# A graph kernel's first attention: the exponential's argument of three units in ten formed by VectorE from two broadcast rows

## The reference

```python
h = (x @ W).reshape(N, H, C)
as_n = (h * a_src).sum(-1)
ad_n = (h * a_dst).sum(-1)
e = jax.nn.leaky_relu(as_n[src] + ad_n[dst], NEG_SLOPE)      # slope 0.2
m = jax.ops.segment_max(e, dst, num_segments=N)
p = jnp.exp(e - m[dst])
s = jax.ops.segment_sum(p, dst, num_segments=N)
alpha = p / (s[dst] + 1e-16)
out = jax.ops.segment_sum(alpha[:, :, None] * h[src], dst, num_segments=N)
```

## Time and profile before

| | |
|---|---|
| median of 3 runs | 3774.85 us (3772.26 to 3774.91) |
| the profiled execution | 3773.97 us, span 3772.4 us |
| first attention's units, from the first weighing to the last eviction | 602.09 to 1079.70 us of the span |
| busy in the whole span | TensorE 93%, VectorE 53%, ScalarE 45%, GpSimd 55% |

### The profile page before, as it was taken

One profiled execution on the slowest core, in us unless ns is written; L12 is line 12 of the kernel. 1 busy time (PEld: TensorE's weight loads), 2 busy tenths in 40 slices (PEclk: granted clock), 3 DMA queues, 4 the chain that ended last, 5 costly groups with the idle time before them and its releaser, 6 DMA issues.

```text
span 3772.4 us, 58635 instructions
## 1 busy us (share of the span) xinstructions
PE 3494.7 (93%) x19026; PEld 2954.7 (78%) x19027; DVE 1984.3 (53%) x2688; ACT 1694.6 (45%) x2961; POOL 2059.4 (55%) x1612
## 2 busy tenths in 40 slices
PE   7998867999988799779998999999999999999898
PEld 4565436999988799623334799999999999999898
DVE  7346888888643544699985442433342424240034
ACT  1114777888843331379994233333333333333221
POOL 7888885666657530000000477777777777776400
PEclk9999998999999999889999999999999999999999
DMA  4342112223143421411103577777777676765501
GB/s 149 108 117 70 33 33 77 79 80 92 53 123 100 129 65 56 137 54 38 42 29 124 187 174 168 171 172 167 174 165 176 164 176 161 180 161 108 104 32 66
DMA packets 171359, 423.60 MB, mean 112 GB/s; under 512 B 39614, under 2 KB 62165, under 8 KB 171222
## 3 DMA queue, kind: packets, MB, share of 16 engines
q0 software_dynamic: 69184, 193.10, 24.5%
q1 hardware_dynamic: 87702, 202.74, 16.5%
q10 hardware_dynamic: 14336, 26.07, 1.9%
HBM read 293.54 MB, written 127.92 MB: 112 GB/s over the span
## 4 chain that ended last, share of the span: by engine, by line
PE 46%; ACT 7%; DVE 2%; issue 2%; DMA 1%; SPq 0%; POOL 0%; ACTq 0%; DVEq 0%; POOLq 0%
PE ps L2156 31%; PE ps L2143 7%; ACT work L1342 4%; ACT ps L1333 3%; PE ps L1746 3%; PE ps L331 2%; PE ps L323 2%; DVE work L1164 1%; PE ps L1279 1%; DVE work L1192 1%; DMA ct<-x_d 0%; ACT work L1352 0%; PE ps L343 0%; DMA acc_d<-ct,relrec 0%; DMA hbuf<-acc_d 0%
## 5 line engine op out<-in xcount | busy, mean ns | idle before, releaser
L2156 PE MATMUL ps<-wsplit,xsplit 128*128 x6840 | 1234.8, 337 | 0.0
L2156 PEld LDWEIGHTS ps<-wsplit,xsplit 128*128 128x128 f32 x6840 | 1180.2, 188 | 0.0
L2196 ACT ACTIVATE ct<-ps,invs 128x768 f32<-128x768 f32 x190 | 171.3, 902 | 919.1 <-PE ps L2156 919.1
L2053 DVE CAST wsplit<-wplain 128x768 fp32r<-128x768 f32 x210 | 157.5, 750 | 804.6 <-PE ps L2156 788.1
L1342 ACT ACTIVATE work<-ps,work 128x418 f32<-128x418 f32 x720 | 438.5, 631 | 109.2 <-PE ps L1252 103.7
L1289 PE MATMUL ps<-hbuf,work 128*128 128x193 f32 x2400 | 455.4, 328 | 15.1 <-DVE work L1206 13.1
L2106 POOL DMA_INDIRECT acc_d<-ct,relrec x190 | 335.6, 1766 | 236.0 <-DMA acc_d<-ct,relrec 185.8
L2085 POOL TENSOR_TENSOR xsplit<-ct,xsplit 128x768 fp32r<-128x768 f32 x190 | 447.8, 2357 | 0.3 <-ACTq L2190 0.2
L1289 PEld LDWEIGHTS ps<-hbuf,work 128*128 128x128 f32 x2400 | 408.3, 190 | 42.4 <-issue 16.8
L1333 ACT ACTIVATE ps<-work,lr 128x418 f32<-128x418 f32 x720 | 431.3, 633 | 6.3 <-DMA work<-lrow_d 6.3
L1192 DVE SCALAR_TENSOR_TENSOR work<-work,cnt 128x1250 f32<-128x1250 f32 x240 | 349.7, 1457 | 135.1 <-ACT work L1342 134.3
(11 more groups left out here) (235 smaller groups left out, 4683.0 us busy)
## 6 DMA issues: line engine op xcount, KB each, us to landing
wplain<-in_L_gnn_W_rel SPq DMA_DIRECT2D x34, 2304.0 KB, 11.5
work<-lrow_d SPq DMA_DIRECT2D x47, 625.0 KB, 3.8
feat_d<-work ACTq DMA_DIRECT2D x30, 386.0 KB, 3.9
hbuf<-feat_d SPq DMA_DIRECT2D x60, 193.0 KB, 2.5
gat_d<-work POOLq DMA_DIRECT2D x12, 960.0 KB, 5.2
xplain<-gat_d SPq DMA_DIRECT2D x30, 384.0 KB, 4.7
work<-xa_d SPq DMA_DIRECT2D x27, 384.0 KB, 3.7
wplain<-x_d SPq DMA_DIRECT2D x20, 384.0 KB, 3.0
```

Of the source, the lines that this page charges most:

```text
L2156: last = pe.matmul(ps[:, 4 + 2 * (u % 2) + h, 0:HALF], x[:, u, c * P:(c + 1) * P], w7[:, bass.ds(base + (lo * KC * D + c * D + h * HALF), ...
```

## The change

In units 3, 5 and 7 of each head of the first attention (`rowwise = (3, 5, 7)`; the second attention gets an empty list) no relu, no shift addition and no PSUM bank are used. VectorE forms the exponential's argument with one operation over 1250 elements, the larger of (row 0 + 0.8 l) and row 1, where row 0 is r minus the maximum's bound and row 1 is 0.8 times the shift, both broadcast over the partitions. ScalarE takes one exponential over the whole unit in place. The two rows come by way of DRAM: `shifts` writes them as a pair of columns with two more small operations, SP stores the pair with one DMA of single numbers in `shift(h)`, and loads two broadcast rows per head. The skipped units' relu passes to the next unit that has one. `larger(q + 1)` stands behind `weigh(q)` and ahead of the maxima.

```diff
+        pair_d = dram("pair_d", (24, 2, NP))
...
+                self.rowwise = rowwise
+                if rowwise:
+                    self.l8 = cv(24 * NT)
+                    self.pair = [cv(2 * NT) for _ in range(2)]
...
+                        self.two_rows = [cv(N), h5(N)]
...
+                    if self.rowwise:
+                        sp.dma_start(pair_d[self.heads_before + h].rearrange("t (j p) -> p t j", p=P), self.pair[h % 2].rearrange("p (t j) -> p t j", t=2),
+                                     allow_slow_non_contiguous=True).then_inc(self.s_c_out, 16)
+                    sp.wait_ge(self.s_c_out, self.at["c_out"] + self.out_parts * (h + 1))
...
+                def two_rows(h):
+
+                    if h:
+                        sp.wait_ge(self.s_pre, self.at_pre + self.rowwise_before(NT * h))
+                    for t in range(2):
+                        sp.dma_start(self.two_rows[t], pair_d[self.heads_before + h, t:t + 1, 0:N].rearrange("t n -> (t n)").partition_broadcast(P))\
+                          .then_inc(self.s_pair_in, 16)
...
                 shift(0)
+                if self.rowwise:
+                    two_rows(0)
                 l_row(2)
                 shift(1)
...
+                    if self.rowwise and h + 1 < H:
+                        two_rows(h + 1)
                     if h + 2 < H:
                         shift(h + 2)
...
+                    if self.rowwise:
+                        step.count(v.scalar_tensor_tensor(self.pair[h % 2][:, 0:NT], self.M, -1.0, lr[:, r0:r0 + NT], ALU.mult, ALU.add))
+                        step(v.tensor_scalar(self.pair[h % 2][:, NT:2 * NT], self.c, 1.0 - SLOPE, None, ALU.mult))
                     v.transpose(self.turned[h % 2], self.parts).then_inc(self.s_c, 1)
+
+                def larger(q):
...
+                    if s == self.rowwise[0]:
+                        v.wait_ge(self.s_pair_in, self.at_pair_in + 32 * (h + 1))
+                    if q >= 3:
+                        v.wait_ge(self.s_agg, self.at["agg"] + (3 if self.narrow else 1) * (q - 2))
+                    v.scalar_tensor_tensor(self.p[q % 3][:, 0:N], self.two_rows[0], self.l8[:, col:col + 1], self.two_rows[1], ALU.add, ALU.max)\
+                     .then_inc(self.s_pre, 1)
...
+                    step.count(v.tensor_scalar(self.l8, lr[:, 0:24 * NT], 1.0 - SLOPE, None, ALU.mult))
...
                     weigh(q)
+                    larger(q + 1)
...
+                    if s in self.rowwise:
+                        return [lambda: None] * 3
...
+                    if q % NT in self.rowwise:
+
+                        col = self.columns[q // NT][0] + q % NT
+                        act.wait_ge(self.s_pre, self.at_pre + self.rowwise_before(q) + 1)
+                        act.activation(self.p[q % 3][:, 0:N], self.p[q % 3][:, 0:N], ACT.Exp, bias=self.l2[:, col:col + 1])\
+                           .then_inc(self.s_exp, 1)
+                        continue
```

More of the change, by code:

```diff
@@ L1027, in build, with __init__ @@
             AHEAD = 4
-            def __init__(self, C, mask, columns, outs, isolated):
+            def __init__(self, C, mask, columns, outs, isolated, rowwise, spare=None):
                 self.C, self.mask, self.columns, self.outs, self.isolated = C, mask, columns, outs, isolated
@@ L1072, in __init__, with plain, exps, rowwise_before @@
                  self.s_primed) = att_sems
+                self.s_pre, self.s_pair_in = s_pre, s_pair_in
+                self.at_pre = att0.rowwise_before(T) if self.narrow else 0
+                self.at_pair_in = 32 * H * bool(att0.rowwise) if self.narrow else 0
+            def plain(self, q):
+                return q - len(self.rowwise) * (q // NT) - sum(s < q % NT for s in self.rowwise)
+            def exps(self, q):
+                return q + 2 * self.plain(q)
+            def rowwise_before(self, q):
+                return q - self.plain(q)
             def row(self, v):
@@ L1376, in build @@
         att0 = Attention(D // 4, mask1v, [((2 * l * 4 + h) * NT, ((2 * l + 1) * 4 + h) * NT) for l in range(3) for h in range(4)],
-                         [(gat_d[l], h) for l in range(3) for h in range(4)], False)
+                         [(gat_d[l], h) for l in range(3) for h in range(4)], False, (3, 5, 7))
         assert att0.used <= WORK - KC * D - RT - 2
@@ L1927, in build @@
         norm6 = Norm()
-        att2 = Attention(D // 12, mask2v, [(h * NT, (12 + h) * NT) for h in range(12)], None, True)
-        parts6 = [m6(2 * D).rearrange("p (u n) -> p u n", u=2), ct[:, :].bitcast(F32)[:, 0:2 * D].rearrange("p (u n) -> p u n", u=2)]
+        parts_res6 = m6(2 * D)
+        att2 = Attention(D // 12, mask2v, [(h * NT, (12 + h) * NT) for h in range(12)], None, True, (), parts_res6[:, 0:N])
+        parts6 = [parts_res6.rearrange("p (u n) -> p u n", u=2), ct[:, :].bitcast(F32)[:, 0:2 * D].rearrange("p (u n) -> p u n", u=2)]
         def sp_parts(sp, j):
```

33 lines of the change are left out of this document (25 added, 8 removed).

## The result

| | before | after |
|---|---|---|
| median | 3774.73 us (3772.26 to 3778.59, 20 runs) | 3782.11 us (3777.13 to 3785.64, 20 runs) |
| the profiled execution | 3773.97, span 3772.4 | 3779.70, span 3778.1 |

The ratio is 1.0018, 95% interval [1.0011, 1.0025]: 7.4 us slower. Forecast were 3765.3 us and at most 3779. The change is small (the bound for "no change" in the prediction is 0.2%, 7.5 us), but it is clear of noise, it goes the other way, and the time lies 3 us above the range.

A forecast was written before the change was run, and what follows sets the result against it. The prediction took TensorE to bound the first attention's heads, with VectorE just keeping up. Gain 17.1 us, less 3.5 in the first head and 4.1 at the start: -9.5 us, so 3765.3 us, range 3759 to 3779.

The forecast's parts named there:

- later pair stores are hidden: Pair stores after the start: their row is first used over 30 us later, so they were counted as costing nothing.
- What bounds the kernel, and what a unit saves: First attention's heads: TensorE sets the 39.41 us period; each unit without shift addition saves 0.53 us, 17.1 us in all.
- VectorE's slack: Heads with maxima: VectorE just keeps up, with about 0.2 us room per `larger` and 0.36 at the head's end.
- VectorE the bound in part: Rival, chance 0.18: each `larger` with signals costs 0.35 us more in the first attention, TensorE stalls, 3770.4 us.
- `larger` slow: Rival, chance 0.12: `larger` takes 2.26 us, kernel 3783 us; slower than before from about 2.0 us per operation.
- The exponential's price: Changed units: ScalarE's one exponential over 1250 elements takes 1.30 us.
- The first head: First attention's first head, bound by VectorE: loses 3.5 us; a longer low clock could add up to 2, taken 0.
- The two rows: The two broadcast rows per head, 625 KB each: their loads are hidden, due at 45 us and issued at about 27.
- The start: Before the first weighing: 4.1 us lost (bounds 0.9 and 22), with the pair store landing after 4.5 us.
- The pair store is slow: Rival, chance 0.12: the pair store takes 10 to 22 us instead of 4.5, kernel 3771 to 3783 us.

The follow-up runs named there:

- the run with two: The change with the pair transposed and stored as four DMAs of 128-byte runs, only units 3 and 7 of each head: 3767.21 us, ratio 0.9981.
- The fourth unit: The change with the pair transposed and stored as 128-byte runs, units 2, 4, 6 and 8 of each head: 3780.68 us, ratio 1.0016.
- two rows loaded once: The change with the pair transposed and stored as 128-byte runs, the two broadcast rows loaded for head 0 only: 3765.96 us, ratio 0.9979.
- store alone: The kernel before plus the two small operations and the single-number pair store in all 12 heads, read by nobody: 3809.93 us, ratio 1.0089.
- forms: The kernel before with pair stores differing by head (full, half, 512 bytes apart, 80-byte runs, none): one execution, 3799.24 us.
- own wait: The change, its single-number store on its own semaphore that only the load of the two rows waits for: 3785.32 us, ratio 1.003.
- spread: The change with each stored number 512 bytes from the next in DRAM, the two rows loaded from other memory: 3763.78 us, ratio 0.9969.
- the cheap store: The change, but VectorE transposes the pair and SP stores it with four DMAs of 128-byte runs: 3765.21 us, ratio 0.9975.

## Why the prediction was wrong

Two steps failed, both on the pair store: its landing at the start, taken as 4.5 us and measured as 14.7, and "later pair stores are hidden", taken as 0 and measured as 7.0 us. The rest of the sum came true.

- **What bounds the kernel, and what a unit saves: right.** Period 37.82 us against 37.82 by TensorE; one unit 0.53 in the run with two. With the store out of the way the heads gained 16.8 to 17.5 us against 17.1.
- **VectorE's slack: right, just.** `larger` is 0.05 us dearer than taken, within the 0.2 of room. The fourth unit, and the 0.09 us of one more transposition, show that the slack was used up. The rivals "VectorE the bound in part" and "`larger` slow" are out: 1.43 us against a turning point of 2.0.
- **The exponential's price: right.** 1.339 us against 1.30 from rows; the estimate by the page "ScalarE: Activation LUTs" of the Trainium skill (its section on what ACT_TABLE_LOAD costs), 1.32, is nearer.
- **The first head: right.** +3.9 against +3.5. The longer stand didn't keep the clock low for longer by any amount that shows: TensorE's mean granted clock in the first head is 0.92 of full speed before and after.
- **The two rows: hidden, right** (two rows loaded once).
- **The start: wrong, the term mis-sized.** I took 4.5 us for the pair store's landing and it took 14 to 15. My bounds, 1.3 and 22.6, held it; the choice between them failed. It rested on the earlier trace rows, where 2362 small packets pass in 2 us. These belong to loads, and a load's packets end in SBUF; this store's packets pass as quickly, and the landing comes 10 us behind them. So the row that fitted best by packets didn't fit in the direction and in where the bytes fall. The 2.2 us so worked out hold for the packets, which pass in 1.6 us (738.11 to 739.74), but not for the landing; written 512 bytes apart, the same numbers land in 5 to 6. The estimate from the Trainium skill leans the same way. The 10.5 ns of its page "DMA: Bandwidth & Descriptors" (bandwidth) are worked out from a load of 64 packets in all, and I counted them for each DMA engine. Counted so, they agree with this trace (1.63 us for the 161 packets of one engine, 10.1 ns each); they price no landing.
- **"Later pair stores are hidden": wrong.** I checked who needs the row (30 us later, true) and which queue stands behind. I didn't ask what a store in flight does to engines that use nothing of it. While it is in flight TensorE's signals arrive up to 3.8 us late in the kernel after (up to 6.7 in others), and ScalarE stands for them: 7.0 us of longer periods in the profiled execution of the kernel after, 20.0 in the kernel before with the store alone. The sum had no term for it.
- **The rival came true in half.** "The pair store is slow", 10 to 22 us and 3771 to 3783, has the right landing and a time that holds the measured 3782, but its sum lacked the stops, so that it holds 3782 only by its wide bounds: with 14.7 in place of 4.5 alone it would be 3775.5. I gave it 0.12 and cut the range at 3779. With a term whose bounds are 20 us apart, no row of the right direction, and a mechanism named in the text itself ("single numbers of neighbouring partitions meet in DRAM"), that was too little.

**Open.** Why TensorE's signals are late. Known: they are late only while a full store is in flight or just behind its landing, though not in all such heads (forms, store alone); whether SP waits for it or not (own wait); not with as many scattered packets (spread). Only TensorE's are late, as far as the records go; some of ScalarE's and VectorE's increments are missing in just the kernels that have full stores (in the kernel after 9 of 249 of ScalarE's relus), so the writing of the trace is disturbed too. The stops need no cause inside ScalarE, as it starts within 0.1 us of the increment. By which way the store holds up the signals, no run shows.

## What to carry to other kernels

Price a store to DRAM by its landing, from a row of a store, never by the packets of a load, and ask where its bytes fall: turn columns into runs first (one small transposition on VectorE, four stores of 128-byte runs: 2.4 us instead of 14.7). A transfer is hidden only if nobody needs it and its being in flight disturbs nobody; look in the trace for a wait whose releaser had ended long before, or is called "remote" in a program on one core, and compare the time of the semaphore's increment with the end of the instruction that makes it. Where an operation is moved to an engine with just enough slack, leave it out of the stage's first head, in which that engine was the bound already.

## What was not expected of the hardware

- One store of 2560 single 4-byte numbers (10 KB), neighbours from different partitions: landed after 14.6 to 18.4 us. 1280: 11.2 to 11.6. 2560, 512 bytes apart: 4.7 to 6.1. 128 runs of 80 bytes: 1.5.
- The DMA engines are idle for some 4 us of this (605 to 609 us) before the landing is reported.
- A load issued on SP's queue behind the store lands behind it: 21 us from the first shift store to the first weighing, with and without a wait.
- During such a store increments of semaphores that TensorE makes arrive up to 6.7 us behind the matmul's end (own wait: ended 829.74, arrived 836.39), and whoever waits for them stands: ScalarE, once VectorE and SP. In the eight kernels without such a store none of them is late by more than 0.02 us.
- GpSimd's store of a head takes 14.1 us to land in the kernel after and 21.2 with the store that SP doesn't wait for (own wait); 5.2 before, 5.3 with the cheap store, 7.0 with the spread one.
